# Values' products of an attention step in two halves, with the maxima products at other places of the step

## What is computed

```python
# b, s, d_model = 4, 1024, 128; h = 16 heads of hd = 8 channels
query = heads(ct_q @ Wu_q_w + Wu_q_b) + heads(_rope(ct_q @ Wq_r_w + Wq_r_b, cos, sin))
key   = heads(ct_kv @ Wu_k_w + Wu_k_b) + heads(_rope(x @ Wk_r_w + Wk_r_b, cos, sin))
value = heads(ct_kv @ Wu_v_w + Wu_v_b)
attn = jnp.einsum('bhqd,bhkd->bhqk', query, key) / sqrt(h + D_KV + D_Q)     # = / 12
attn = jax.nn.softmax(attn, axis=-1)
out = jnp.einsum('bhqk,bhkd->bhqd', attn, value)
return out.transpose(0, 2, 1, 3).reshape(b, s, d_model) @ Wo_w + Wo_b
```

## Time and profile before

| | us |
|---|---|
| time, median of 3 runs | 2005.73 |
| lowest and highest of them | 2004.09, 2005.89 |
| span of the profiled execution, first to last instruction | 2004.5 |
| first scores of the attention to the first scores of its last group | 625.66 |
| PE busy over the span | 1788.9 (89%) |
| DVE busy over the span | 1459.2 (73%) |
| ACT busy over the span | 1092.4 (54%) |

### The profile page before, as it was taken

One profiled execution on the slowest core, in us unless ns is written; L12 is line 12 of the kernel. 1 busy time (PEld: TensorE's weight loads), 2 busy tenths in 40 slices (PEclk: granted clock), 3 DMA queues, 4 the chain that ended last, 5 costly groups with the idle time before them and its releaser, 6 DMA issues. The chain is left out here.

```text
span 2004.5 us, 34034 instructions
## 1 busy us (share of the span) xinstructions
PE 1788.9 (89%) x12761; PEld 670.6 (33%) x12761; DVE 1459.2 (73%) x3121; ACT 1092.4 (54%) x1386; POOL 644.9 (32%) x776
## 2 busy tenths in 40 slices
PE   6878799999999999999599888888888888889897
PEld 3535333333333333333333332111211211112465
DVE  5866666666666667663444689999999999994743
ACT  4312244454455445545324158878887878887432
POOL 0033445445555555432224113203302500001153
PEclk8987999999999999999799899999999999999798
DMA  4000000000000000000121101211221212220114
GB/s 137 1 1 1 1 21 25 23 24 23 23 24 23 34 24 24 33 24 23 24 111 54 62 26 69 74 44 44 81 81 45 86 65 63 82 81 7 63 35 145
DMA packets 56673, 91.80 MB, mean 46 GB/s; under 512 B 21989, under 2 KB 30565, under 8 KB 56381
## 3 DMA queue, kind: packets, MB, share of 16 engines
q1 hardware_dynamic: 54940, 85.94, 12.4%
q0 software_dynamic: 1280, 2.62, 0.5%
q10 hardware_dynamic: 288, 1.05, 0.2%
HBM read 46.23 MB, written 38.51 MB: 42 GB/s over the span
## 5 line engine op out<-in xcount | busy, mean ns | idle before, releaser
L1853 DVE TENSOR_REDUCE h_m_half<-h_ps_max 128x1 f32<-128x512 f32 x1024 | 635.8, 682 | 32.4 <-PE h_ps_max L1460 29.7
L1709 ACT ACTIVATE h_P<-h_ps_st 128x1024 f32<-128x1024 f32 x512 | 497.8, 1023 | 86.6 <-PE h_ps_st L1476 84.0
L929 PE MATMUL l_ps_st<-l_Q,l_K 64*128 64x512 f32 (+3 forms) x1536 | 310.3, 498 | 4.2 <-DMA l_Q<-l_m_row 2.0
L1089 ACT ACTIVATE l_P<-l_ps_st 128x1024 f32<-128x1024 f32 (+3 forms) x256 | 207.7, 834 | 192.7 <-PE l_ps_st L929 192.0
L1180 DVE CUSTOM_DVE_ANT_0 l_masked<-l_ps_t,l_mask 128x384 bf16<-128x384 f32 (+3 forms) x512 | 229.3, 485 | 63.7 <-PE l_ps_t L883 63.6
L1486 PE MATMUL h_ps_o<-h_P,h_V 128*9 128x512 f32 x2048 | 267.7, 595 | 0.7 <-ACT h_P L1709 0.5
L1460 PE MATMUL h_ps_max<-h_K,h_Q 48*128 48x512 bf16 x1024 | 201.0, 389 | 66.7 <-DVE h_m_half L1853 64.7
L1183 DVE TENSOR_REDUCE l_m_half<-l_ps_t 128x1 f32<-128x512 f32 x256 | 164.5, 685 | 69.7 <-PE l_ps_t L883 68.3
L1476 PE MATMUL h_ps_st<-h_Q,h_K 51*128 51x512 bf16 x1024 | 167.4, 379 | 14.9 <-ACT h_P L1709 11.0
L1460 PEld LDWEIGHTS h_ps_max<-h_K,h_Q 48*128 48x128 bf16 x1024 | 49.2, 93 | 387.1 <-DVE h_m_half L1853 372.5
L1757 POOL CAST h_m_parts<-h_m_neg 128x16 bf16<-128x16 f32 x32 | 6.3, 198 | 517.3 <-DVE h_m_neg L1817 517.3
(11 more groups left out here) (469 smaller groups left out, 2416.2 us busy)
## 6 DMA issues: line engine op xcount, KB each, us to landing
sums<-l_o SPq DMA_DIRECT2D x15, 512.0 KB, 2.7
sums<-h_o SPq DMA_DIRECT2D x15, 512.0 KB, 2.6
h_K<-k_parts SPq DMA_DIRECT2D x32, 192.0 KB
h_Q<-q_parts SPq DMA_DIRECT2D x32, 192.0 KB
y_rows<-zero SPq DMA_DIRECT2D x8, 512.0 KB, 4.9
c_W<-c_W SPq DMA_DIRECT2D x32, 128.0 KB, 2.1
c_W<-in_W SPq DMA_DIRECT2D x16, 256.0 KB, 4.0
c_back<-y_rows SPq DMA_DIRECT2D x16, 256.0 KB, 5.6
```

What stands on the lines that cost most here:

```text
L929: last = pe.matmul(ps_st[x % 2][:, a, 0:w], K[n // NG % 2][rows, kt * 128:(kt + 1) * 128], Q[n % NQ][rows, c, p, q0 - c * CH:q0 - c * CH + ...
L1089: act.activation(P[e % PR][:, :, 0:w], ps_st[slot["s", n, i, p] % 2][:, :, 0:w], ACT.Exp, scale=0.125).then_inc(consumed, 1)
L1709: act.activation(P[e % PR][:, :, :], ps_st[x % 2][:, :, :], ACT.Exp, scale=1.0 / 12.0).then_inc(consumed, 1)
L1853: dve.tensor_reduce(m_half[:, half, 2 * p + a, qt:qt + 1], ps_max[:, t % NB, :], AX.X, ALU.max, negate=True)\
```

## The change

`values` gets a parameter `side` and makes the products of 256 of the 512 columns. Both sides are called, and the waits stand at side 0 alone, the increment of `pv_done` at side 1 alone. The start flag stands at side 0 of the first tile of keys, and the stop flag at side 1 of the last. The pairs of maxima change places: the first stands between the two scores in every step, the second between the two sides of the values, and is left out there in the steps of `SKIP`. A third pair still stands behind a product.

```diff
--- before.py
+++ after.py
@@ -1477,15 +1477,17 @@
                                      Q[n % NBUF][rows, p, c * CH:(c + 1) * CH], start=True, stop=True)
                 last.then_inc(st_ready, 1)
 
-            def values(n, i):
-                kt, b, g = i % KT, n // NG, n % NG
-                pe.wait_ge(consumed, item["s", n, i, 1] + 1)
-                if kt == 0 and (n or i):
-                    pe.wait_ge(o_kept, 2 * n + i // KT)
+            def values(n, i, side):
+                kt, b, g, cols = i % KT, n // NG, n % NG, slice(side * CH // 2, (side + 1) * CH // 2)
+                if side == 0:
+                    pe.wait_ge(consumed, item["s", n, i, 1] + 1)
+                    if kt == 0 and (n or i):
+                        pe.wait_ge(o_kept, 2 * n + i // KT)
                 for j in range(HG):
-                    last = pe.matmul(ps_o[32 * j:32 * j + M, :], V[b % 2][:, kt, g * HG + j, :],
-                                     P[(2 * (n * NI + i) + j // 2) % PR][:, j % 2, :], start=(kt == 0), stop=(kt == KT - 1))
-                last.then_inc(pv_done, 1)
+                    last = pe.matmul(ps_o[32 * j:32 * j + M, cols], V[b % 2][:, kt, g * HG + j, :],
+                                     P[(2 * (n * NI + i) + j // 2) % PR][:, j % 2, cols], start=(kt == 0 and side == 0), stop=(kt == KT - 1 and side == 1))
+                if side:
+                    last.then_inc(pv_done, 1)
 
             def normalise(kind, b, half):
                 to = free_slot(item[kind, b])[:, :, :].rearrange("p a c -> p (a c)")
@@ -1579,16 +1581,15 @@
                     if i in TURNS and 2 * n + 1 + TURNS.index(i) < 2 * NGR:
                         turn(2 * n + 1 + TURNS.index(i))
                     key = AT.get((n, i))
-                    follows = (n, i - 1) in AT
                     scores(n, i, 0)
-                    if follows:
-                        next_maxima()
+                    next_maxima()
                     scores(n, i, 1)
-                    if not follows and (n, i) not in SKIP:
+                    if n + i:
+                        values(n if i else n - 1, (i - 1) % NI, 0)
+                    if (n, i) not in SKIP:
                         next_maxima()
                     if n + i:
-                        values(n if i else n - 1, (i - 1) % NI)
-                    next_maxima()
+                        values(n if i else n - 1, (i - 1) % NI, 1)
                     if key and key[0] == "out":
                         output(key)
                         next_maxima()
@@ -1602,7 +1603,8 @@
                         out_last(0, True)
                     if n == NGR - 1 and i in LN_AT:
                         ln_center_early(*LN_AT[i])
-            values(NGR - 1, NI - 1)
+            for side in range(2):
+                values(NGR - 1, NI - 1, side)
             pe.wait_ge(ln_moved, 4)
             out_last(1, False)
             spread_last_sums(1)
```

## The result

| | before | after |
|---|---|---|
| median of 16 runs each, us | 2005.75 | 2010.41 |
| lowest and highest | 2003.95, 2007.79 | 2007.48, 2014.64 |
| span of the profiled execution | 2004.5 | 2007.1 |
| first scores of group 0 to those of group 15 | 625.66 | 629.45 |
| PE busy over the span | 1788.9 | 1825.2 |

The ratio is 1.0025, with a 95% interval of 1.0017 to 1.0032: slower by a quarter of a per cent, 4.7 us. The time lies inside the stated range of 2001.0 to 2013.5, but 3.2 us above the forecast of 2007.2, and just past the bound of 0.2% inside which I had put 65% of the chances; "slower" had 22%.

The account below looks back on a forecast made before the run. DVE's reductions of the maxima were the bound, but held off their own pace. Groups without a product -2.9, with four +3.6, with one +0.6, last steps +0.2: +1.5 us on 2005.73 gives 2007.2; range 2001.0 to 2013.5.

Parts of the forecast that it names:

- Plain steps: Steps without product or turn: PE gaps of 1.09 and 1.10 under DVE's 1.20, step 2.47 to 2.39 us.
- Groups without a product: Groups 2, 3, 12, 13: from 39.9 to 39.1 us, -0.8 each but -0.5 for group 2, -2.9 in all.
- The rival that DVE does not reach its pace: Slower: if a pair takes 1.20 us or more in steady steps, gains are lost, +5.9 us, 2013; chance 0.10.
- The price of the cut: Values on PE: a half taken as 0.44 us; change-over and way back cost 0.20 us of PE a step.
- the rival of the dearer cut: Slower: weights not hidden in the second pass make each half 0.09 longer, 7 us more, 2014; chance 0.10.
- single matmuls: Slower by far: eight matmuls of 256 columns take 0.64, not 0.44 us; plain step 2.59, 2035; chance 0.02.
- Steps with a `ka`, `ct` or `out`: Product step plus the one behind: 1.93 us from second to third pair, sum 6.54 to 6.70, a loss of 0.16.
- The rival by which C would catch up: Faster: the third pair, behind a product, catches up; twelve groups gain 0.2 each, -5.3 us, 2000.4; chance 0.12.
- Steps with an `x` or `y`: The 12 products of 64 rows: a loss a little less than 0.16 us each.
- The turns: SKIP steps, second pair of step 4 to that of step 8: 8.94 to 9.04 us, twice in four-product groups.
- a sign of being wrong: A new wait of PE for ACT or for the parts of the maxima at the head of a half; no size given.
- the plain steps of groups with four products: Two plain steps in each of groups 0, 1, 4, 5, 8, 9: some 0.2 us taken off each group's loss.

Follow-up runs that it names:

- experiment 7: The changed kernel with each reduction of the maxima reading 448 of the 512 columns; 1989.66 us, ratio 0.9925 against the changed kernel.
- Experiment 1: The changed kernel with its pairs of maxima back at the places of the kernel before, the two value halves behind one another; 2009.62 us, ratio 1.0024.
- Experiment 3: The changed kernel with, in the 30 product steps, the product and the pair behind it ahead of the second half of the values; 1993.57 us, ratio 0.9941.
- Experiment 8: The kernel of Experiment 3 with the next group's maxima rows ahead of the load of the group after it on SP's queue; 1993.01 us, ratio 0.994.

## Why the prediction was right and where it was off

**Plain steps: right.** 2.39 us, both gaps under DVE's pace, by 0.09 to 0.10 as experiment 7 shows. Groups without a product gave 2.8 us, 2.9 forecast; three of them ran at 38.83 to 38.95 us, a little under the 39.1 taken for DVE's own work, and that made up for group 2, which came out 0.7 over its forecast. The rival that DVE does not reach its pace falls.

**The price of the cut: right.** A half is 0.44 us. Experiment 1 adds that cut values with nothing between them cost at most 0.01 us a step, and 9 columns of weights behave as the 17 of the earlier trace rows: the rival of the dearer cut falls, and so does that of single matmuls. The Trainium skill, page TensorEngine Tiling (Array Packing), section Instruction Overhead, gives each matmul an overhead of some 60 cycles. Taken as a time that every further matmul adds, as the prediction took it, the eight more rows of a step would cost 0.2 us (an estimate from that figure at 2.4 GHz); for these matmuls, on four tiles of the array in turn, experiment 1 shows 0.01 at most.

**Steps with a `ka`, `ct` or `out`: right in the mechanism.** 1.93 between B and C, and 6.68 for 6.70 over two steps. From first scores to first scores of two steps on, the loss of 0.16 measured 0.13 to 0.24 in eleven of the twelve with `ka` or `ct`, 0.17 in the mean. The first product of group 0 lost 0.78 instead, and why only this one did is open. The five with `out` in groups 0 to 14 lost 0.24 each. Experiment 3 shows that this gap is what the change loses by: without it the same cut gains 12 us on before. The rival by which C would catch up falls with it.

**Steps with an `x` or `y`: a little over, not under.** The prediction put these 12 in brackets as "a little less" than 0.16 us. Such a step and the one behind it are together 6.63 us where they were 6.44 (means of the 12), 0.19 more. PE across such a product, before and then after:

```profile
1387.56 0.39 PE L1460 MATMUL h_ps_max<-h_K,h_Q 48*128 48x512 bf16 x2
1387.79 0.59 PE L2133 MATMUL h_ps_st<-c_W,h_Wu 64*128 64x512 f32 x1
...
1388.73 0.39 PE L1460 MATMUL h_ps_max<-h_K,h_Q 48*128 48x512 bf16 x2
```
```profile
1387.31 0.39 PE L1460 MATMUL h_ps_max<-h_K,h_Q 48*128 48x512 bf16 x2
1387.63 0.62 PE L1487 MATMUL h_ps_o<-h_P,h_V 128*9 128x256 f32 x8
1388.18 0.69 PE L2134 MATMUL h_ps_st<-c_W,h_Wkv 64*128 64x512 f32 x1
...
1389.14 0.39 PE L1460 MATMUL h_ps_max<-h_K,h_Q 48*128 48x512 bf16 x2
```

Before, the product followed its pair after 0.23, what scores take behind a pair; by the rows both use no more than half of the array's rows (48*128 and 64*128), which I take for the reason. Now the values stand between, and a change over and one back come with them. B to C went from 1.17 to 1.83, by 0.66, where the products of 128 rows, which paid for a change before too, went up by 0.55. Most of that 0.11 does not reach the step, whose sum grew by 0.19 against the 0.17 of `ka` and `ct`: the 12 cost 2.3 us in all, 0.4 more than 12 times 0.16, a third of the 1.3 by which groups 1, 5 and 9 exceeded their forecast.

**The turns: right in sum, unequal in place.** B of step 4 to B of step 8 is 8.97 (1353.54 to 1362.51), before 8.94, forecast 9.04. For the second turn of the group, B of step 12 to B of step 0 of the next group is 9.05 (1375.87 to 1384.92), before 8.84. Together 0.24 for a forecast of 0.2. The second one ends at the head of the next group, so its cost is counted in groups 1, 2, 5, 6, 9 and 10.

**Landing of the maxima rows: left out.** By the view of the waits over the stage, before and then after (us, times, longest):

```profile
PE h_ps_st L1476 <- DMA h_Q<-h_m_row: 1.7, 6, 0.7
```
```profile
PE h_ps_st L1476 <- DMA h_Q<-h_m_row: 3.9, 11, 0.8
```

The wait that stood in the earlier trace rows with 0.17 us grew from 1.7 to 3.9 us in all. Most of it falls at the heads of groups, and the longest ends group 2:

```profile
1299.76 0.39 PE L1476 MATMUL h_ps_st<-h_Q,h_K 51*128 51x512 bf16 x2 [0.82 <-DMA h_Q<-h_m_row]
```

On SP the four small transfers for it stand behind two loads of the queries, before and then after:

```profile
1292.32 1.43 SPq L2125 DMA_DIRECT2D h_Q<-q_parts  x2
1294.72 3.06 SPq L1372 DMA_DIRECT2D h_Q<-h_m_row  x4
```
```profile
1293.09 1.43 SPq L2127 DMA_DIRECT2D h_Q<-q_parts  x2
1294.62 3.06 SPq L1372 DMA_DIRECT2D h_Q<-h_m_row  x4
```

The four were not issued later than before: in both kernels they follow within 0.03 us on ACT's copy of the row (which ended at 1294.69 and 1294.60). What changed is that the two loads, of 192 KB each, went out 0.8 us later and stand right ahead of them. Before, the next scores came 4.28 us behind the first of the four and did not wait; after, 5.14, with the wait. I had named such a wait as a sign of being wrong, but gave it no price.

**Where the missing 2.6 us of the stage are.** Group 2 is 0.7 over its forecast and group 6 0.3, and there the waits for the rows grew by 0.8 and 0.3 us. Experiment 8 shows, for the kernel of experiment 3, that such waits are lost time in these groups. Groups 1, 5 and 9 are 1.3 over: 0.4 by `x` and `y`, and 0.6 by the 0.2 us that the prediction took off in each for two plain steps. Step 0 is no plain step there but the tail of the turn ahead of it, with 2.25 us where it was 2.04, and step 8 belongs to a turn too. Group 0 is 0.6 over, by its first product. Groups 3, 12 and 13 are 0.6 under, and the others together 0.2 over. This is reckoned from the trace of one execution of each kernel; no experiment took these parts out one by one in the kernel after.

**Which rival came true: none.** The time came out slower by the forecast's own mechanism, with several small terms on the loss's side too small: the waits for the rows (no price), the plain steps of groups with four products (0.2 us gained was reckoned in each; it is 0.1 in groups 4 and 8 and none in 1, 5 and 9), `out` (0.24 for 0.16), `x` and `y` (0.19 for less than 0.16) and the first product (0.78 for 0.16). The forecast was 1.5 us and the medians moved by 4.7. That the time still lies in the stated range owes as much to the range as to the sum. The profiled execution was also matched to the median wrongly: I set a span of 2004.5 against a median of run times. A run's time is 1.8 over its span (2008.87 and 2007.1 after), so that profile stood near 2006.3, and 1.2 under the median it was not. The sum of +1.5 was added to the median, so this did not move the forecast. From the attention on, after's profile is 4.4 us longer (1.75 + 2.6): 3.4 to the end of its steps and 0.9 behind, in a part that the change leaves alone. That 0.9 stays open; it is inside the 2 us by which the ten profiles differ there.

## What to carry to other kernels

Where one engine's work is fed by another in equal portions, what counts is each gap between two portions against the consumer's pace: cutting the filler equalises the gaps in plain steps (2.47 to 2.39 us), but every step that carries something extra must be re-planned too, with the extra in a gap of its own and the filler in the next. Here that is one move of two lines and worth 17 us, the difference between a quarter of a per cent lost and 0.6% won. When a forecast is a small difference of a gain and a loss, price the special steps one kind at a time, and give a number to each transfer that now lands just in time.

## What was not expected of the hardware

- Splitting values of 512 columns by 9 columns of weights in two costs at most 0.01 us for 16 rows in place of 8, if nothing stands between the halves; a pair between them costs a change over and back, 0.09 to 0.11 each.
- A float32 product of 64 rows follows a bf16 pair of 48 rows after 0.23 us, one of 128 rows or the values after 0.32. Such a product is a free neighbour of a pair and a dear one of the values.
- Up to the attention, where no edit reaches, ten profiles differ by 7 us (1166.6 to 1173.8), and behind it by 2; the granted clock of the first 200 us, 0.86 to 0.91, does not order them. In the kernel after, single runs on either side of a mean clock of 0.967 stand 4 us apart. A difference of a few us is to be read from the stage that the change touches, and times are to be compared at like clocks.
